# A graph attention network on one core: pauses ahead of every fifth gather, the carries moved by 32x32 transposes, merged loads, and the spread from two digits

## The chip, the cores and the metric

The kernel runs on one NeuronCore of a Trainium2 chip. The metric is the device time of one execution in microseconds, the median of the runs. The engines are PE (TensorE, with its weight loads shown as PEld), DVE (VectorE), ACT (ScalarE), POOL (GpSimd) and SP (SyncE, which only issues DMAs here).

## The reference

6250 nodes with 128 features and 206250 edges, sorted by destination (100000 edges both ways and a loop at each node). Three graph attention layers, then one layer of sums over edge attributes:

```python
xl = (x @ Wl + bl).reshape(n, heads, outc)
e_feat = leaky_relu(xl[src] + (x @ Wr + br).reshape(n, heads, outc)[dst], 0.2)
logits = einsum('ehc,hc->eh', e_feat, att)
m = segment_max(logits, dst);  a = exp(logits - m[dst])
out = segment_sum(xl[src] * a[:, :, None], dst) / segment_sum(a, dst)   # then bias, layer norm, relu
```

Two layers have four heads, the third one has one. The last part takes `segment_sum(edge_attr, col)` (96 wide), divides by the counts, joins it to the node's features, and applies two products with a batch norm between them. Both results are added to the input and normalized.

## The kernel before, in words

**Data.** The edges lie in 62 chunks of 3328, each of 26 tiles of 128 edges (`TILES`). An item is a chunk with a window of 128 destination nodes; a table made at the start (`item_tab`) lists them, 62 for each layer in this trace. Each layer has a node phase (it writes the tables `xl_tab` and `xr_tab` of 132 columns and the state) and an edge stage over the items. The stages lie at 132 to 2716, 2871 to 5359 and 5507 to 7998 us.

**An item.** GpSimd gathers 128 rows of `xl_tab` by source for each tile, 26 indirect DMAs (L633) of 66 KB each, into `xl_g`, which has two buffers. PE spreads the destinations of a tile over 128 partitions (L683: a row of `sel` picks tile t of `rel`, the destinations less the window's base, in bf16); ScalarE turns them into a one-hot tile `ST` (L879, L881) and, from the other side, `S` (L854, L857). PE multiplies `ST` by the window's `xr_w` (L694), VectorE adds the gathered rows (z, L1133), takes the relu times the attention vector (L1140), and sums per head (L1149, L1163): the logits.

**The maxima.** The logits are transposed (L701) so that each tile and head is one of 104 rows. Scans give the running maxima from both ends of a row (L1187, L1188). A segment can run through several tiles, so the last column of the upward and the first of the downward scan go through PE to one partition (L704, L705), two scans of 104 elements join them over the tiles (L1195, L1196) with penalties that ScalarE made from `tile_ends`, two sums give the carries (L1199, L1200), PE brings them back to 104 partitions (L708, L709), and VectorE copies them out of PSUM (L1206). They start the scans L1208 and L1210, whose result PE transposes (L712). Then come `shifted` (L1216), the exponential (L891), the messages (L1226) and their sums on PE (L727), and the merge into the state.

**Order.** Items are pipelined: a step of each engine opens one item (to its logits) and closes the one before it, and prepares the next. Groups of four tiles (`GROUPS`, seven of them, the last of two) interleave opening and closing: `runs` at group 0, `carries` and `maxima` at 1, `shift` at 2, `message` from 2 on (`SUMS_AT`). The order on each queue is written out by hand; semaphores join the queues.

**Waits of GpSimd.** The buffer of an item is free once the messages of the item two before it are made, group by group: GpSimd waits for `msg_done[g]` ahead of each group. Ahead of groups 1 to 6 it also pauses until all but the last gather of the group before have landed (`most_gathered`, L630). A small `sem_inc(spacer)` stands behind each wait.

**Loads.** SP loads for the item after the next (`load_item`, L515 to L530): three tables by partition (`idx`, `dst_e`, `dst_next`), the destinations by row four times (`dst_r`, one for each head), the ends of each tile, the window's node numbers, and `xr_w`.

Of the kernel before, what the change touches and what calls it, by code (L numbers as in the profile page):

```python
# [25 lines left out]
P = 128  # L26
# [21 lines left out]
NG = len(GROUPS)  # L48
SUMS_AT = {2: (0,), 3: (1, 2), 4: (3, 4), 5: (5, 6)}
EA_CUTS = (0, 4, 9, 16, TILES)  # L50
LH = TILES * HEADS

# [33 lines left out]
ITEM_DMAS = 5 + HEADS  # L86
# [3 lines left out]
def gnn_program(nc, x, src_t, dst_t, next_t, dst, edge_attr, node_id, Wl, bl, Wr, br, att, c, g, be,  # L90
                u, W1, b1, gamma, beta, W2, b2, out):
    ctx = ExitStack()
    with ctx:
# [16 lines left out]
        item_tab = scratch("item_tab", (MAX_ITEMS, 2), I32)  # L110

# [40 lines left out]
        idx = sb("idx", [P, 2, TILES], I32)  # L152
        dst_e = sb("dst_e", [P, 2, TILES], I32)
        dst_next = sb("dst_next", [P, 2, TILES], I32)
        dst_r = sb("dst_r", [LH, 2, P], I32)
        tile_ends = sb("tile_ends", [1, 2, TILES, 2], I32)
# [6 lines left out]
        rel = sb("rel", [TILES, 2, P], BF16)  # L163
        sel = sb("sel", [TILES, TILES, P], BF16)
        neg_p = sb("neg_p", [P, 1])
        distT = sb("distT", [P, 2, 4 * P])
# [7 lines left out]
        logit = sb("logit", [P, 2, LH])  # L174
        seg_last = sb("seg_last", [P, TILES])
        row_eq = sb("row_eq", [LH, P])
        row_pen = sb("row_pen", [LH, P + 1])
        tile_eq = sb("tile_eq", [1, TILES + 1])
        tile_one = sb("tile_one", [1, TILES])
        through = sb("through", [1, 2, TILES])  # L180
        through_pen = sb("through_pen", [1, 2, LH])
        enter_pen = sb("enter_pen", [1, 2, LH])
        run_up = sb("run_up", [LH, P])
        run_down = sb("run_down", [LH, P])
        open_max = sb("open_max", [1, 2, LH + 2])
        carry = sb("carry", [1, 2, LH])
        carry_col = sb("carry_col", [LH, 2])
        up = sb("up", [LH, P])
        seg_max = sb("seg_max", [LH, P])
# [56 lines left out]
        b_cut = s_flat[0:PARTS, F + 2 * b_all:F + 4 * b_all].bitcast(BF16)  # L246
        bn = sb("bn", [P, 8, 2])
# [5 lines left out]
        lt_ps = PS[0:LH, 4, 0:P]  # L253
        spread_ps = PS[:, 7, :]
        mb_ps = PS[:, 4, 128:128 + LH]
        open_ps = [PS[0:1, 4, 232 + d * LH:232 + (d + 1) * LH] for d in range(2)]
        carry_ps = PS[0:LH, 4, 440:442]
        agg_ps = PS[:, 5, 0:MSG]
        ea_ps = PS[:, 6, 0:D_EDGE]
        hT_ps = flat[:, 0:NROWS]  # L260
# [1166 lines left out]
```

## Time and profile before

| | us |
|---|---|
| median of 3 runs (lowest, highest) | 8285.53 (8282.69, 8302.3) |
| the profiled execution | 8275.22 |
| its span, first to last instruction | 8273.2 |
| PE busy | 5435.2 (66%) |
| POOL busy | 4817.3 (58%) |
| DVE busy | 4759.2 (58%) |
| ACT busy | 4443.8 (54%) |
| first gather | 131.9 |

Busy time is that of the instructions' records; waiting, register work and DMA issue are not counted. The gap behind a gather is therefore idle time, whatever it is for. A wait "<- remote" or "<- issue" is one whose release the records do not show; PE's own ends are modelled. A gather's record is the making of its descriptors on GpSimd, not the transfer. Matmuls of f32 data have two records each.

### The profile page before, as it was taken

To read this page: it belongs to the slowest core of one execution; us is meant where nothing else is said; L and a number is where in the kernel's file an instruction comes from. 1 tells how busy PE (TensorE), PEld (TensorE's weight loads), DVE (VectorE), ACT (ScalarE), POOL (GpSimd) and SP (SyncE) were. 2 spreads that over 40 slices of the span, in tenths; PEclk is the share of its full clock that TensorE was granted. 3 is DMA by queue.
4 is the path that set the end of the run, shared out by engine and by line. 5 is a ranking of instruction groups with operands and counts; after the bars stand their busy time and mean duration, and the time that the engine had idled before them with its cause. 6 is when DMAs were issued, how large, how long until landed. Compare 5 with 4: busy or idle time off the path is not lost.

```text
span 8273.2 us, 114570 instructions
## 1 busy us (share of the span) xinstructions
PE 5435.2 (66%) x30380; PEld 4591.5 (55%) x30380; DVE 4759.2 (58%) x13239; ACT 4443.8 (54%) x10857; POOL 4817.3 (58%) x4843
## 2 busy tenths in 40 slices
PE   5777777777777765666656665666566666566656
PEld 3666666666666455555555554535555555455544
DVE  3555565555565555656556655655556556565556
ACT  3555555555555454555555655545555556555546
POOL 2666666666666166666666666626666666666640
PEclk8777777777777666666666666656666666666666
DMA  4333333333332322222222222242222222222221
GB/s 115 86 84 84 85 85 84 78 90 77 84 92 76 89 53 53 53 52 51 53 53 53 54 53 52 49 88 53 52 54 54 53 54 53 53 50 53 53 49 47
DMA packets 469478, 538.50 MB, mean 65 GB/s; under 512 B 196815, under 2 KB 377749, under 8 KB 461495
## 3 DMA queue, kind: packets, MB, share of 16 engines
q0 software_dynamic: 154752, 327.15, 17.7%
q1 hardware_dynamic: 314679, 210.82, 9.7%
q8 instruction: 18, 0.29, 0.0%
q14 instruction: 29, 0.24, 0.0%
HBM read 485.07 MB, written 52.43 MB: 65 GB/s over the span
## 4 chain that ended last, share of the span: by engine, by line
another core or an unknown queue 20%; POOL 18%; issue 18%; DVE 15%; PE 14%; ACT 9%; DMA 5%; DVEq 0%; POOLq 0%; ACTq 0%; SPq 0%
POOL xl_g L633 18%; DMA xl_g<-xl_tab,idx 4%; PE PS L694 3%; PE PS L727 3%; ACT dist L854 3%; DVE z L1133 3%; DVE am L1140 2%; PE PS L666 2%; DVE msg L1226 2%; ACT distT L879 2%; PE PS L720 2%; DVE relu_logit L1149 1%; PE PS L683 1%; DVE relu_logit L1152 1%
## 5 line engine op out<-in xcount | busy, mean ns | idle before, releaser
L633 POOL DMA_INDIRECT xl_g<-xl_tab,idx x4836 | 4816.5, 996 | 3179.9 <-issue 2328.3
L727 PE MATMUL PS<-msg,S 128*128 128x137 f32 x9672 | 1699.2, 338 | 895.9 <-DVE msg L1226 588.1
L879 ACT ACTIVATE distT<-PS,neg_p 128x512 f32<-128x512 f32 x1302 | 847.1, 651 | 2521.4 <-remote 1821.0
L727 PEld LDWEIGHTS PS<-msg,S 128*128 128x128 f32 x9672 | 1530.5, 236 | 1022.8 <-issue 943.8
L694 PE MATMUL PS<-xr_w,ST 128*128 128x132 f32 x9672 | 2032.1, 373 | 86.0 <-DVE z L1133 44.4
L1133 DVE TENSOR_TENSOR z<-PS,xl_g 128x528 f32<-128x528 f32 x1302 | 863.6, 663 | 1977.4 <-remote 1251.5
L694 PEld LDWEIGHTS PS<-xr_w,ST 128*128 128x128 f32 x9672 | 1820.8, 275 | 153.6 <-issue 128.6
L854 ACT ACTIVATE dist<-node_row,neg_dst 128x128 f32<-128x128 f32 x4836 | 1534.5, 386 | 0.0
L683 PE MATMUL PS<-rel,sel 26*128 26x128 bf16 x4836 | 640.9, 267 | 1058.2 <-ACT distT L879 593.9
L683 PEld LDWEIGHTS PS<-rel,sel 26*128 26x128 bf16 x4836 | 348.5, 111 | 1348.4 <-ACT distT L879 675.5
L1140 DVE SCALAR_TENSOR_TENSOR am<-z,att_relu 128x512 f32<-128x512 f32 x1302 | 852.6, 655 | 6.5
L881 ACT ACTIVATE ST<-distT 128x512 f32<-128x512 f32 x1302 | 780.4, 599 | 41.6
L857 ACT ACTIVATE S<-dist 128x512 f32<-128x512 f32 x1302 | 780.4, 599 | 41.2
L1226 DVE TENSOR_TENSOR msg<-xl_g,msg 128x512 f32<-128x512 f32 x1302 | 791.2, 642 | 0.6 <-ACT msg L891 0.6
L1149 DVE TENSOR_REDUCE relu_logit<-am 128x16 f32<-128x512 f32 x868 | 554.1, 638 | 17.1
L720 PE MATMUL PS<-ea,S 128*128 128x96 f32 x3224 | 551.6, 336 | 5.6 <-issue 5.2
L720 PEld LDWEIGHTS PS<-ea,S 128*128 128x128 f32 x3224 | 512.3, 246 | 31.8 <-issue 24.1
L708 PE MATMUL PS<-ones,carry 1*104 1x1 f32 x372 | 88.0, 303 | 530.4 <-DVE carry L1200 294.2
L891 ACT ACTIVATE msg<-shifted 128x104 f32<-128x104 f32 x186 | 56.6, 304 | 622.0 <-DVE shifted L1216 361.7
L708 PEld LDWEIGHTS PS<-ones,carry 1*104 1x104 f32 x372 | 72.8, 250 | 570.4 <-DVE carry L1200 319.5
L1195 DVE TENSOR_TENSOR_SCAN open_max<-through_pen,PS 1x104 f32<-1x104 f32 x186 | 66.5, 357 | 493.7 <-remote 445.0
L1152 DVE TENSOR_REDUCE relu_logit<-am 128x4 f32<-128x512 f32 x434 | 276.9, 638 | 8.5
(198 smaller groups left out, 4005.1 us busy)
## 6 DMA issues: line engine op xcount, KB each, us to landing
xl_g<-xl_tab,idx POOLq DMA_INDIRECT x4836
ea<-edge_attr SPq DMA_DIRECT2D x62, 1248.0 KB
xr_w<-xr_tab SPq DMA_DIRECT2D x186, 66.0 KB
dst_r<-dst SPq DMA_DIRECT2D x744, 13.0 KB
node_row<-node_id SPq DMA_DIRECT2D x186, 64.0 KB
xl_tab<-xl_g SPq DMA_DIRECT2D x30, 330.0 KB, 3.7
xr_tab<-xl_g SPq DMA_DIRECT2D x30, 330.0 KB, 5.0
st_old<-state SPq DMA_DIRECT2D x124, 68.0 KB
```

The lines of the kernel that those rows point to most:

```text
L633: pool.indirect_dma_start(xl_g[:, q, t, :], None, xl_tab[:, :], bass.IndirectOffsetOnAxis(idx[:, q, t:t + 1], 0))\
L683: last = pe.matmul(spread_ps[:, n * P:(n + 1) * P], sel[:, t, :], rel[:, q, :], start=True, stop=True)
L694: last = pe.matmul(zp[(q + g) % 2][:, n, :], ST[:, t, :], xr_w[:, q, :], start=True, stop=True)
L720: pe.matmul(ea_ps, S[:, q, t, :], ea[:, q, t, :], start=t == 0, stop=t == TILES - 1)
L727: last = pe.matmul(agg_ps, S[:, q, t, :], msg[:, t, :], start=t == 0, stop=t == TILES - 1)
L854: last = act.activation(dist[:, (q + g) % 2, m, :], node_row[:, q, :], ACT.Abs, bias=neg_dst[:, q, t:t + 1])
L857: act.activation(S[:, q, GROUPS[g][0]:GROUPS[g][0] + n, :], dist[:, (q + g) % 2, 0:n, :], ACT.Relu, bias=1.0, scale=-1.0)\
L879: act.activation(distT[:, (q + g) % 2, 0:n], spread_ps[:, 0:n], ACT.Abs, bias=neg_p[:, 0:1]).then_inc(spread_read, 1)
L881: act.activation(ST[:, GROUPS[g][0]:GROUPS[g][-1] + 1, :].rearrange("p t n -> p (t n)"), distT[:, (q + g) % 2, 0:n], ACT.Relu, bias=1.0, s ...
L1133: dve.tensor_tensor(out=z[:, (q + g) % 2, 0:n, :], in0=zp[(q + g) % 2][:, 0:n, :], in1=xl_g[:, q, a:a + n, :], op=ALU.add).then_inc(z_done ...
L1140: dve.scalar_tensor_tensor(am[:, (q + g) % 2, 0:n, :], z[:, (q + g) % 2, 0:n, 0:F], 0.0, att_relu[:, stage, :].unsqueeze(1).to_broadcast([ ...
L1226: dve.tensor_tensor(out=msg[:, a:a + n, 0:F].rearrange("p t (h f) -> p t h f", h=HEADS), in0=xl_g[:, q, a:a + n, 0:F].rearrange("p t (h f) ...
```

## The change

It does six things together.

1. GpSimd waits for landed gathers ahead of tiles 5, 10, 15, 20 and 25 (`PACE = 5`) and not ahead of tiles 4, 8, ..., 24. The gathers are counted in ten sets (`SETS`) cut at both the pauses and the groups; each pause waits for the sets that end before the gather still in flight. The waits for messages stay ahead of tiles 0, 4, ..., 24. `dynamic_dma_scratch_size` is set to 8192 where the default was 16384.
2. The logits have 128 rows instead of 104 (32 for each head, the last six zero). The carries go by VectorE's 32x32 transposes: two of [128, 32] bring the ends to where each head's 26 tiles lie along a row, the scans and sums run over 26 elements on all partitions, and one of [128, 64] takes the carries back. PE's four products and the copy out of PSUM are gone.
3. The flags of tile ends come from `dst_r` by a copy and one transpose; `tile_ends` is gone.
4. The spread is one product for a group, of weights 128 and 1 (`digit_w`, 2x128) by two bf16 digits of the destinations (2x512). The digits are made for all edges at the start and stored in `digit_tab`; `sel` and `rel` are gone, and the window's base moves into the bias of L879 (`neg_node`).
5. The loads of an item are `edges` (three tables in one), `dst_r` (one table of 128 rows), `digits`, `node_row` and `xr_w`.
6. ScalarE makes the penalties in four activations, not five.

```diff
+PACE = 5
+PAUSES = range(PACE, TILES, PACE)
+STEPS = sorted({PACE * b - 1 for b in range(1, len(PAUSES) + 1)} | {g[-1] + 1 for g in GROUPS})
+SETS = [range(a, b) for a, b in zip([0] + STEPS[:-1], STEPS)]
+SET_OF = [m for m, tiles in enumerate(SETS) for t in tiles]
+PAUSE_FOR = {t: [m for m, tiles in enumerate(SETS) if max(t - PACE - 1, 0) <= tiles[-1] < t - 1] for t in PAUSES}
-                        for g, tiles in enumerate(GROUPS):
-                            pool.wait_ge(msg_done[g], pairs * (2 * stage) + 2 * i + (q + 1))
-                            pool.sem_inc(spacer, 1)
-                            if g:
-                                pool.wait_ge(most_gathered[g - 1], (pairs * (2 * stage) + 2 * i + (q + 1)) * (16 * (len(GROUPS[g - 1]) - 1)))
+                        v = pairs * (2 * stage) + 2 * i + (q + 1)
+                        for t in range(TILES):
+                            for m in PAUSE_FOR.get(t, ()):
+                                pool.wait_ge(gathered[m], v * (16 * len(SETS[m])))
                                 pool.sem_inc(spacer, 1)
-                            for t in tiles:
-                                pool.indirect_dma_start(xl_g[:, q, t, :], None, xl_tab[:, :],
-                                                        bass.IndirectOffsetOnAxis(idx[:, q, t:t + 1], 0))\
-                                    .then_inc(gathered[q][g] if g == NG - 1 or t == tiles[-1] else most_gathered[g], 16)
+                            if t % 4 == 0:
+                                pool.wait_ge(msg_done[t // 4], v)
+                                pool.sem_inc(spacer, 1)
+                            pool.indirect_dma_start(xl_g[:, q, t, :], None, xl_tab[:, :],
+                                                    bass.IndirectOffsetOnAxis(idx[:, q, t:t + 1], 0))\
+                                .then_inc(last_gathered[q] if SET_OF[t] == len(SETS) - 1 else gathered[SET_OF[t]], 16)
...
-                        for n, t in enumerate(GROUPS[g]):
-                            last = pe.matmul(spread_ps[:, n * P:(n + 1) * P], sel[:, t, :], rel[:, q, :], start=True, stop=True)
-                        last.then_inc(spread, 1)
+                        a, n = GROUPS[g][0] * P, len(GROUPS[g]) * P
+                        pe.matmul(spread_ps[:, 0:n], digit_w[:, :], digits[:, q, a:a + n], start=True, stop=True).then_inc(spread, 1)
...
+            dve.wait_ge(dst_in, 16)
+            dve.tensor_scalar(all_digit, all_dst, DIGIT.bit_length() - 1, None, ALU.arith_shift_right).then_inc(digits_made, 1)
+            dve.tensor_scalar(all_dst, all_dst, DIGIT - 1, None, ALU.bitwise_and).then_inc(digits_made, 1)
+            dve.wait_ge(digits_made, 2)
+            dve.tensor_copy(all_digits[0], all_digit).then_inc(digits_made, 1)
+            dve.tensor_copy(all_digits[1], all_dst).then_inc(digits_made, 1)
...
-                    first, last = tile_ends[:, q, :, 0], tile_ends[:, q, :, 1]
+                    dve.tensor_copy(ends[:, :, :], dst_r[:, q, 0:P:P - 1].unsqueeze(2).to_broadcast([P, 2, SQ])).then_inc(flag_done[2], 1)
+                    dve.wait_ge(flag_done[2], v * 3 - 2)
+                    dve.transpose(ends_T[:, :, :].rearrange("p a t -> p (a t)"), ends[:, :, :].rearrange("p a t -> p (a t)")).then_inc(flag_done[2], 1)
...
+                    dve.wait_ge(runs_done, v)
+                    dve.transpose(run_T[:, 0, :], run_up[:, P - SQ:P])
+                    dve.transpose(run_T[:, 1, :], run_down[:, 0:SQ]).then_inc(open_done, 1)
                     dve.wait_ge(open_done, v)
-                    dve.tensor_tensor_scan(open_max[:, 0, 1:LH + 1], through_pen[:, 0, :], open_ps[0], -BIG, ALU.add, ALU.max)
+                    dve.tensor_tensor_scan(open_max[:, 0, 1:TILES + 1], through_pen[:, 0, :], run_T[:, 0, 0:TILES], -BIG, ALU.add, ALU.max)
...
+                    dve.wait_ge(carry_done, v)
+                    dve.transpose(carry_T[:, :, :].rearrange("p a t -> p (a t)"), carry[:, :, :].rearrange("p a t -> p (a t)")).then_inc(carryT_done, 1)
...
-                    dve.tensor_copy(carry_col[:, :], carry_ps).then_inc(carrycol_done, 1)
...
-    nc = bacc.Bacc("TRN2", target_bir_lowering=False, num_devices=1)
+    nc = bacc.Bacc("TRN2", target_bir_lowering=False, num_devices=1, dynamic_dma_scratch_size=8192)
```

## Rows read from the trace of the kernel before

**Rows 1.** the cores: span and mean granted TensorE clock
```profile
core 0: 8273.2 us, clock 0.696
```

**Rows 2.** by stretch: PE, PEld, DVE, ACT, POOL busy, granted clock, DMA share, GB/s
```profile
132.00:2716.00 2584.00, 1908.96 (x11753) 1698.22 (x11754) 1457.05 (x4148) 1362.35 (x3325) 1602.16 (x1612) 0.76 0.32 84
2871.00:5359.00 2488.00, 1541.83 (x8606) 1315.33 (x8606) 1454.48 (x4044) 1404.28 (x3375) 1609.05 (x1612) 0.67 0.24 53
```

**Rows 3.** GpSimd's group of gathers: count, busy us, mean ns, idle and what ended it
```profile
L633 POOL DMA_INDIRECT xl_g<-xl_tab,idx x4836 | 4816.5, 996 | 3179.9 <-issue 2328.3 <-DMA xl_g<-xl_tab,idx 686.4 <-DVE msg L1226 165.2
```

**Rows 4.** GpSimd's waits (us, times, longest): first stage, second stage, whole run
```profile
POOL xl_g L633 <- DMA xl_g<-xl_tab,idx: 349.2, 202, 5.8
...
POOL xl_g L633 <- DMA xl_g<-xl_tab,idx: 176.7, 147, 2.8
...
POOL xl_g L633 <- DVE msg L1226: 165.2, 36, 15.9
```

**Rows 5.** timeline of GpSimd: start, us, instruction, idle before
```profile
4058.26 0.94 POOL L633 DMA_INDIRECT xl_g<-xl_tab,idx  x1 [0.30 <-issue]
4060.44 0.95 POOL L633 DMA_INDIRECT xl_g<-xl_tab,idx  x1 [1.23 <-DMA xl_g<-xl_tab,idx]
4062.52 0.95 POOL L633 DMA_INDIRECT xl_g<-xl_tab,idx  x1 [1.13 <-issue]
```

**Rows 6.** the chain of work in order of time, around one item's end
```profile
4079.23 0.02 POOLq L631
4079.25 0.76 issue
...
4080.74 0.02 POOLq L628
...
4082.75 0.02 POOLq L628
...
4083.01 1.01 POOL xl_g L633
```

**Rows 7.** groups by line and shape: VectorE around the carries, and its longest
```profile
L1133 DVE TENSOR_TENSOR z<-PS,xl_g 128x528 f32<-128x528 f32 x1116 | 783.8, 702 | 1811.6 <-remote 1108.2 <-DMA xl_g<-xl_tab,idx 409.9 <-PE PS L694 224.7
...
L1195 DVE TENSOR_TENSOR_SCAN open_max<-through_pen,PS 1x104 f32<-1x104 f32 x186 | 66.5, 357 | 493.7 <-remote 445.0 <-PE PS L705 26.3 <-issue 22.3
...
L1123 DVE TENSOR_SCALAR neg_dst<-dst_e 128x26 f32<-128x26 int32 x186 | 33.0, 177 | 0.0
...
L1206 DVE COPY carry_col<-PS 104x2 f32<-104x2 f32 x186 | 28.8, 155 | 120.4 <-remote 101.0 <-PE PS L709 13.4 <-issue 6.0
...
L1140 DVE SCALAR_TENSOR_TENSOR am<-z,att_relu 128x512 f32<-128x512 f32 x1302 | 852.6, 655 | 6.5
...
L1226 DVE TENSOR_TENSOR msg<-xl_g,msg 128x512 f32<-128x512 f32 x1302 | 791.2, 642 | 0.6 <-ACT msg L891 0.6
```

**Rows 8.** timeline of PE and VectorE, from the product to the scan
```profile
4024.22 0.55 PE L705 MATMUL PS<-ident,run_down 104*1 104x104 f32 x2
...
4033.66 0.36 DVE L1195 TENSOR_TENSOR_SCAN open_max<-through_pen,PS 1x104 f32<-1x104 f32 x1 [7.75 <-remote]
```

**Rows 9.** windows on GpSimd: gathers (x) between unplanned gaps of 1.13 us
```profile
3959.34:4062.52 103.18, 63.54 (x67) 0.68 0.23 52
4062.52:4160.02 97.50, 63.98 (x64) 0.68 0.25 54
4160.02:4259.23 99.21, 66.27 (x66) 0.72 0.24 52
```

**Rows 10.** timeline of VectorE and GpSimd, a message beside a gather
```profile
4073.62 1.28 DVE L1226 TENSOR_TENSOR msg<-xl_g,msg 128x512 f32<-128x512 f32 x2
...
4073.83 1.29 POOL L633 DMA_INDIRECT xl_g<-xl_tab,idx  x1 [1.38 <-DMA xl_g<-xl_tab,idx]
```

**Rows 11.** the copy at the start, and a store (KB, us to landing)
```profile
L1033 DVE CAST sel<-ident 26x3328 bf16<-26x3328 f32 x1 | 1.9, 1880 | 0.0
...
xr_tab<-xl_g SPq DMA_DIRECT2D x30, 330.0 KB, 5.0
```

More of the change, by code:

```diff
@@ L51 @@
 LH = TILES * HEADS
+SQ = 32
+LP = SQ * HEADS
 NB = 5
@@ L173, in gnn_program @@
         relu_logit = sb("relu_logit", [P, LH])
-        logit = sb("logit", [P, 2, LH])
+        logit = sb("logit", [P, 2, LP])
         seg_last = sb("seg_last", [P, TILES])
[L176 to L189, printed above, removed]
+        row_eq = sb("row_eq", [LP, P])
+        row_pen = sb("row_pen", [LP, P + 1])
+        ends = sb("ends", [P, 2, SQ])
+        ends_T = sb("ends_T", [P, 2, SQ])
+        tile_eq = sb("tile_eq", [P, TILES + 1])
+        tile_one = sb("tile_one", [P, TILES])
+        through = sb("through", [P, 2, TILES])
+        through_pen = sb("through_pen", [P, 2, TILES])
+        enter_pen = sb("enter_pen", [P, 2, TILES])
+        run_up = sb("run_up", [LP, P])
+        run_down = sb("run_down", [LP, P])
+        run_T = sb("run_T", [P, 2, SQ])
+        open_max = sb("open_max", [P, 2, TILES + 2])
+        carry = sb("carry", [P, 2, SQ])
+        carry_T = sb("carry_T", [P, 2, SQ])
+        up = sb("up", [LP, P])
+        seg_max = sb("seg_max", [LP, P])
         shifted = sb("shifted", [P, LH])
@@ L283, in gnn_program @@
         state_stored = sem("state_stored")
-        most_gathered = sems("most_gathered", NG - 1)
-        gathered = [sems(f"gathered{q}_", NG) for q in range(2)]
+        gathered = sems("gathered", len(SETS) - 1)
+        last_gathered = sems("last_gathered", 2)
         spacer = sem("spacer")
@@ L469, in _ @@
             sp.wait_ge(table_in, 16)
+            sp.wait_ge(digits_made, 4)
+            for w in range(2):
+                sp.dma_start(digit_tab[w].rearrange("c (h e) -> (c h) e", h=2), all_digits[w]).then_inc(digits_out, 16)
+            sp.wait_ge(digits_out, 32)
             pairs = sp.value_load(pairs_i[0:1, 1:2], min_val=MIN_PAIRS, max_val=MAX_PAIRS)
@@ L743, in pe_step @@
                                 spread_group(opens, g + 2)
-                        if closes and g == 0:
-                            close("open")
-                        if closes and g == 1:
-                            close("carry")
                         if closes and g == 2:
```

114 lines of the change are left out of this document (56 added, 58 removed).

## The prediction

> **What bounds the kernel now.** I read the clock and span first [rows 1], then busy time by stage [rows 2]. No engine is full: in the first edge stage PE is busy for 74% of the stretch, GpSimd for 62%. Busy time hides the bound here, because GpSimd's own gaps are part of its work. The group of gathers shows it [rows 3]: 4836 gathers of 0.996 us and 3179.9 us of idle time, of which only 165.2 us ended on VectorE's messages. So the third view is what GpSimd waits for [rows 4], and the fourth their order in time [rows 5, 6]. A gather follows the one before it after 0.30 us. At a pause (it waits until all but the last of the group's gathers have landed) the gap is about 1.13, at 4060.44 it is 1.23 us: 0.35 to 0.45 us until the wait has passed, then 0.76 us from there to the next gather. The reader is to see that a gather is 1.25 us of GpSimd whatever the data, that 26 of them and 6 pauses are 26 x 0.996 + 20 x 0.30 + 6 x 1.16 = 38.9 us, and that a stage of 2488 us is 62 such items of 40.1 us. GpSimd's issue is the bound. Other engines matter where they keep it waiting: 36 times, 4.6 us each, 15.9 us at most, nearly always ahead of an item's first gather [rows 4].
>
> **Pauses, six to five in an item.** Before, GpSimd waits ahead of tiles 4, 8, ..., 24; after, ahead of 5, 10, 15, 20, 25. Each still leaves one gather in flight, so each costs what it costs now. In stage 0, 202 gaps ended on a landing and lasted 349.2 / 202 = 1.73 us; the other 170 of its 62 x 6 pauses took 1.13 us; the mean is 1.46, so one pause less saves 1.16 us an item, 72 us in the stage. In stage 1, 147 gaps took 176.7 / 147 = 1.20 us and 225 took 1.13: 1.16, less 0.30 is 0.86 us, and 107 us for the 124 items of two such stages. Together **-179 us**; the low end is 186 x 0.83 = -154 (every pause at its shortest, 1.13 less 0.30). The message waits stay ahead of tiles 0, 4, ..., 24, and now mostly stand between two gathers with no pause beside them. Such a wait costs nothing if it has passed: at 4080.74 and 4082.75 two of them run beside the gathers of 4080.01 and 4081.26, and the next gather starts at 4083.01, 0.30 us behind the last one's end [rows 6]. That VectorE waits for two sets of gathers in three groups is a 0.05 us step beside idle time of its own (44% of stage 0, [rows 2]), so nothing; if that cover were gone it would be 0.15 us an item.
>
> **The carries.** Before, VectorE's two scans over the open runs wait for a PE product, the carries go back through PE, and a copy brings them out of PSUM. VectorE sat idle 493.7 us ahead of the scan at L1195, 2.65 us an item, and 120.4 us ahead of the copy at L1206, 0.65 us [rows 7]; in the item of [rows 8] the product's record ends at 4024.77 and the scan starts at 4033.66. After, VectorE transposes the ends itself: three transposes and 26-element scans and sums in place of 104-element ones. I price a transpose as the 128x26 operation at L1123, 0.18 us; three of these, two scans and two sums of about 0.2 are some 1.3 us against five operations of 0.16 to 0.36 us now, so VectorE's own work is unchanged and 3.3 us of waiting goes. The spread loses 19 of its 26 matmuls an item and PE's four carry products go; PE's results come late in such stretches (the 8.9 us above), so I add 1 us for the shorter queue, an estimate. GpSimd comes 0.96 us earlier. The first message is then 3.3 + 1 - 0.96 = 3.4 us earlier against the gather that waits for it. With 36 waits spread evenly from 0 to 9.2 us (mean 4.6), a share (1 - 3.4 / 9.2)^2 = 0.40 stays, so of the 154 us that they cost over a plain gap 0.6 goes: **-95 us**. Ends: -154 (all goes), and +35 (nothing goes and each wait grows by the 0.96 us that GpSimd is early). What is late next is GpSimd's own issue.
>
> **The smaller descriptor area.** The area for gather descriptors is set to 8192 bytes a partition, half of the default. The trace has gaps of 1.13 us behind a gather that is followed by no pause, as at 4062.52 [rows 5], and they come back every 64 to 67 gathers [rows 9]: 65 on average, of which the rows are three of the four that follow 3959.34. That does not fit the loop (52 gathers) but would fit an area that fills. 4836 / 65 is 74 of them. If half the area fills twice as often, 75 more come, of which a fifth fall on a pause and are hidden: 75 x 0.8 x 0.83 = **+49 us**. No row shows that the area is the cause; the ends are 0 and 75 x 0.83 = +62. I take the price, since the period has no other match.
>
> **The shared port.** Gathers of 0.95 us stretch where VectorE multiplies the messages, both inputs in SBUF: 1.29 us at 4073.83 beside L1226 [rows 10]. Over the run the stretch is 4816.5 - 4836 x 0.95 = 222 us, beside 791.2 + 852.6 us of the two such groups L1226 and L1140 [rows 3, 7], 0.14 for each us. The change adds some 0.9 us an item of SBUF-to-SBUF work (three transposes, the copy of the ends, two scans that read PSUM before): 186 x 0.9 x 0.14 = **+23 us**, ends 0 and +60 (the 0.34 us by which that gather grew are 0.36 us for each us of it, for all of the 167 us added). The Trainium skill, GPSIMD Engine Reference, section "Key points", says that GpSimd shares its SBUF interfaces with VectorE and contends with instructions in a 2-port mode or with two SBUF inputs. The trace agrees for two inputs (1.29 against 0.95 us); by the rule the transposes and copies might be free or dear according to their mode, which no row here shows, and the sum would lie between 0 and the +60 above. It speaks against this change.
>
> **Start and loads.** The load of all destinations, four VectorE operations over 1664 columns and two stores stand ahead of the first round. VectorE drops the 1.88 us copy of 3328 columns at L1033 [rows 11], about half of what it gains at the same rate (4 x 0.94 = 3.8), and waits for weights anyway. SP waits for stores of 413 KB, priced as the 330 KB store of 5.0 us [rows 11]: **+5 us**, ends 0 and +10. The item's loads fall from ten DMAs to five. They are issued an item ahead, so 40 us of gathers hide them before and after, nothing is gained; without that cover the 2 to 3 us that SP saves would count. ScalarE drops one of five small activations off the path.
>
> **Sum.** 8275.2 us (the profiled execution; span 8273.2 and 2.0 around it) - 179 - 95 + 49 + 23 + 5 = 8078. The median of the runs is 10.3 us above the profiled one: 8088, so I predict **8090 us**, 2.4% faster. With each doubtful term halfway to its ends, one or two at a time, this case covers 8030 to 8150.
>
> **Rivals.** *All waits go* (0.20): messages are never late, the area costs nothing, the port little: 8275 - 179 - 154 + 5 + 10 = 7957, up to 8030. For it: the carries' round trip is most of what delays them. Against: the longest wait is 15.9 us, more than any part removed. *Only the pause* (0.18): PE's lateness is not cured by removing round trips, because the lateness sits in the products that remain; the waits stay or grow: 8275 - 179 + 35 + 49 + 23 + 5 + 10 = 8218, from 8150. For it: z at L1133 also waits for PE after its record ends, and it stays (1108.2 us, [rows 7]). *Slower* (0.07): a message wait apart from a pause drains GpSimd's queue and costs the 0.76 us restart too. Tiles 4, 8, 12, 16 and 24 then add five gaps: 186 x 5 x 0.83 = +772, 8088 + 772 = 8860 us. It decides as soon as more than about 1.3 of these five restart in an item (the 195 us gained over 186 x 0.83). Against it: [rows 6], where two such waits pass under a gather; it is kept because no row shows three gathers, a wait and a pause in this order. *The gain is eaten* (0.05): port and area at their dear ends and waits that grow: 8275 - 154 + 35 + 62 + 60 + 10 + 10 = 8298, or within 0.3% of it. PE falling to its lower clock with less work (0.67 of full speed already in stage 1, [rows 2]) would act through late messages, so it is part of the second rival.
>
> **Numbers.** The forecast has 0.50. The range 7960 to 8200 holds it, nearly all of the first rival's and two thirds of the second's time, and leaves out about 0.2. A measurement of this kernel can tell 0.3% (25 us) from no change. Faster 0.88, same 0.05, slower 0.07.
>
> **What would show it.** Five gaps over 1 us in an item's gathers, ahead of the second gather of every fifth; items of stage 1 near 39.0 us; 0.30 us behind message waits; fewer than 25 waits on VectorE's message and under 80 us in them; the unplanned gaps every 32 or so gathers; gathers of 1.00 us on average; first gather 5 us later. It would go wrong if gaps stand at tiles 4, 8, 12 as well, if the message waits do not fall, or if the mean gather grows past 1.02 us.

## The result, and the profile of the changed kernel

| | before | after |
|---|---|---|
| median of 4 runs each, us | 8293.92 (8282.69 to 8314.43) | 8778.46 (8747.18 to 8810.17) |
| ratio, 95% interval | | 1.058 (1.054 to 1.062) |
| profiled span, us; granted clock | [rows 1] | 8745.1; 0.679 |

The change made the kernel 5.8% slower, where 2.4% faster was forecast; 8778 us lies far outside the range. I read the changed kernel in the order in which I read the one before. Its span and clock, against [rows 1]:

```profile
core 0: 8745.1 us, clock 0.679
```

Busy time by stretch (the two stretches of [rows 2] at their new places; PE, PEld, DVE, ACT, POOL, granted clock, DMA share, GB/s):

```profile
144.00:2862.00 2718.00, 1803.60 (x9991) 1556.46 (x9992) 1457.18 (x4366) 1319.16 (x3240) 1578.20 (x1612) 0.73 0.30 80
3029.00:5680.00 2651.00, 1482.44 (x6859) 1196.06 (x6859) 1447.25 (x4246) 1354.45 (x3267) 1582.97 (x1612) 0.65 0.22 50
```

Every engine has less to do or as much, and both stages are longer, by 134 and 163 us. So nothing became busier; something waits more. GpSimd's group, against [rows 3], and its waits over the whole run (us, times, longest), against [rows 4]:

```profile
L652 POOL DMA_INDIRECT xl_g<-xl_tab,edges x4836 | 4739.6, 980 | 3736.8 <-issue 2258.3 <-DVE msg L1250 979.9 <-DMA xl_g<-xl_tab,edges 495.9
...
POOL xl_g L652 <- DVE msg L1250: 979.9, 131, 18.3
```

The waits on VectorE's message went from 165.2 us in 36 to 979.9 in 131. The pauses are as the change says. The timeline of GpSimd shows them five gathers apart, each 1.1 to 1.2 us:

```profile
4068.57 0.94 POOL L652 DMA_INDIRECT xl_g<-xl_tab,edges  x1 [1.18 <-DMA xl_g<-xl_tab,edges]
4069.82 0.94 POOL L652 DMA_INDIRECT xl_g<-xl_tab,edges  x1 [0.30 <-issue]
...
4073.57 0.95 POOL L652 DMA_INDIRECT xl_g<-xl_tab,edges  x1 [0.30 <-issue]
4075.73 0.94 POOL L652 DMA_INDIRECT xl_g<-xl_tab,edges  x1 [1.21 <-issue]
```

In the kernel before they are four apart:

```profile
4004.02 0.94 POOL L633 DMA_INDIRECT xl_g<-xl_tab,idx  x1 [1.11 <-DMA xl_g<-xl_tab,idx]
...
4009.87 0.95 POOL L633 DMA_INDIRECT xl_g<-xl_tab,idx  x1 [1.08 <-DMA xl_g<-xl_tab,idx]
```

The message waits inside an item now mostly stand between two gathers that are 0.30 us apart (18 longer gaps away from the pauses, in 186 items), so the rival *Slower* with its five restarts an item did not happen. Summed over the gathers' starts and ends, the idle time inside the items fell by 230 us (2535 to 2305), the gathers themselves by 77 (4816.5 to 4739.6), and the idle time ahead of an item's first gather grew by 776 (514 to 1290). That one sum is the loss. (It has the turns between stages in it.) Who makes the first message late shows in VectorE's groups, by line and shape:

```profile
L1151 DVE TENSOR_TENSOR z<-PS,xl_g 128x528 f32<-128x528 f32 x1116 | 784.6, 703 | 2568.9 <-remote 2197.3 <-PE PS L712 186.4 <-DMA xl_g<-xl_tab,edges 97.8
...
L1219 DVE TENSOR_TENSOR_SCAN open_max<-through_pen,run_T 128x26 f32<-128x26 f32 x186 | 39.6, 213 | 6.3
```

The scan of the carries waits for nothing any more (493.7 us in [rows 7], 6.3 now). But z, the operation that takes PE's products out of PSUM, waits 2197.3 us for something called remote; for z at L1133 that was 1108.2 in [rows 7]. The timeline shows what it is:

```profile
4028.23 0.60 PE L702 MATMUL PS<-digits,digit_w 2*128 2x512 bf16 x1 [2.48 <-issue]
4028.89 2.13 PE L712 MATMUL PS<-xr_w,ST 128*128 128x132 f32 x8
...
4031.06 0.95 POOL L652 DMA_INDIRECT xl_g<-xl_tab,edges  x1 [1.15 <-issue]
...
4032.82 0.69 ACT L884 ACTIVATE distT<-PS,neg_node 128x512 f32<-128x512 f32 x1 [2.16 <-remote]
4032.85 0.71 DVE L1151 TENSOR_TENSOR z<-PS,xl_g 128x528 f32<-128x528 f32 x1 [3.23 <-remote]
```

PE's spread ends at 4028.83 and its eight products at 4031.02; ScalarE, which waits for the first, and VectorE, which waits for the second, both go on at 4032.8, 4.0 and 1.8 us later (ScalarE had been idle for the last 2.16 us of this), within 0.03 us of each other, and behind a pause of GpSimd. PE's results, or word of them, come late, and here two of them at once. It is the lateness of [rows 8] (8.9 us), which I had called PE's own. The chain of waits gives it a name of its own; by engine, of the changed kernel:

```profile
another core or an unknown queue 34%; DVE 20%; PE 16%; ACT 16%; issue 11%; POOL 1%; DMA 1%; DVEq 1%; SPq 0%; ACTq 0%; POOLq 0%
```

The program runs on one core, so no other core can release anything. The same line of the kernel before, which was there to be read before I predicted:

```profile
another core or an unknown queue 20%; POOL 18%; issue 18%; DVE 15%; PE 14%; ACT 9%; DMA 5%; DVEq 0%; POOLq 0%; ACTq 0%; SPq 0%
```

The word remote proves nothing by itself: it only says that no record names what released the instruction. That the results are late shows in the starts of what waits for them. Where ScalarE's distT had waited for more than 1 us, it started 2.5 us behind the end of the last product of the spread at the median in the kernel before, and 3.2 us in the changed one.

### The profile page after: what moved, and what is told of

The parts are those of the page before. It is cut to its first block, busy times and chain, and to the rows that moved or that the text cites. A ratio compares the mean times of both kernels' runs of the same rounds, so it can differ in the third digit from the quotient of the medians.

```text
span 8745.1 us, 105988 instructions
## 1 busy us (share of the span) xinstructions
PE 5223.6 (60%) x25358; PEld 4225.2 (48%) x25358; DVE 4790.9 (55%) x13989; ACT 4347.3 (50%) x10671; POOL 4740.5 (54%) x4843
## 3 DMA queue, kind: packets, MB, share of 16 engines
q0 software_dynamic: 154752, 327.15, 16.7%
## 4 chain that ended last, share of the span: by engine, by line
another core or an unknown queue 34%; DVE 20%; PE 16%; ACT 16%; issue 11%; POOL 1%; DMA 1%; DVEq 1%; SPq 0%; ACTq 0%; POOLq 0%
ACT dist L861 6%; PE PS L738 4%; ACT distT L884 4%; PE PS L712 4%; DVE z L1151 3%; DVE am L1158 3%; DVE msg L1250 3%; PE PS L731 3%; ACT ST L886 2%; PE PS L685 2%; DVE relu_logit L1167 2%; PE PS L702 2%; ACT S L864 1%; DVE relu_logit L1170 1%
## 5 line engine op out<-in xcount | busy, mean ns | idle before, releaser
L652 POOL DMA_INDIRECT xl_g<-xl_tab,edges x4836 | 4739.6, 980 | 3736.8 <-issue 2258.3
L884 ACT ACTIVATE distT<-PS,neg_node 128x512 f32<-128x512 f32 x1302 | 846.1, 650 | 3339.8 <-remote 2533.0
L738 PE MATMUL PS<-msg,S 128*128 128x137 f32 x9672 | 1733.6, 342 | 1121.1 <-DVE msg L1250 647.2
L738 PEld LDWEIGHTS PS<-msg,S 128*128 128x128 f32 x9672 | 1562.8, 240 | 1293.3 <-issue 1187.2
L702 PE MATMUL PS<-digits,digit_w 2*128 2x512 bf16 x1302 | 641.4, 493 | 1960.8 <-ACT distT L884 1110.4
L702 PEld LDWEIGHTS PS<-digits,digit_w 2*128 2x128 bf16 x1302 | 124.1, 95 | 2280.3 <-ACT distT L884 1250.7
L731 PEld LDWEIGHTS PS<-ea,S 128*128 128x128 f32 x3224 | 545.7, 261 | 41.7 <-issue 41.7
L1167 DVE TENSOR_REDUCE relu_logit<-am 128x16 f32<-128x512 f32 x868 | 556.5, 641 | 17.1
L1259 DVE TENSOR_SCALAR some<-PS 128x1 f32<-128x1 f32 x186 | 29.4, 158 | 461.3 <-remote 404.1
L1181 DVE TENSOR_TENSOR logit<-relu_logit,z 128x16 f32<-128x16 f32 x1302 | 228.8, 176 | 0.1
L685 PE MATMUL PS<-w_lr,n_hT 128*128 128x264 f32 x300 | 173.4, 678 | 0.0
```

The lines of the kernel that those rows point to most:

```text
L652: pool.indirect_dma_start(xl_g[:, q, t, :], None, xl_tab[:, :], bass.IndirectOffsetOnAxis(idx[:, q, t:t + 1], 0))\
L702: pe.matmul(spread_ps[:, 0:n], digit_w[:, :], digits[:, q, a:a + n], start=True, stop=True).then_inc(spread, 1)
L731: pe.matmul(ea_ps, S[:, q, t, :], ea[:, q, t, :], start=t == 0, stop=t == TILES - 1)
L738: last = pe.matmul(agg_ps, S[:, q, t, :], msg[:, t, :], start=t == 0, stop=t == TILES - 1)
L884: act.activation(distT[:, (q + g) % 2, 0:n], spread_ps[:, 0:n], ACT.Abs, bias=neg_node[:, q:q + 1]).then_inc(spread_read, 1)
```

## The experiments

The kernels of the experiments ran in five sessions, each on one chip, one kernel after the other. (The expectations call a session a call.) Ratios are to the kernel before, timed in the same session.

| session | kernel | median, us | ratio (95%) | waits on messages, us, times | PE's results |
|---|---|---|---|---|---|
| 1, before 8220 | b_area8192 | 8163 | 0.994 (0.992 to 0.996) | 0 | late |
| | b_pace5 | 8696 | 1.060 (1.056 to 1.065) | 805.9, 156 | late |
| | a_pace4 | 8354 | 1.018 (1.014 to 1.021) | 0 | late |
| | a_area16128 | 8517 | 1.036 (1.033 to 1.040) | 749.8, 98 | late |
| 2, before 8063 | b_nopause | 9794 | 1.214 (1.208 to 1.220) | 2804.0, 209 | late |
| | b_memset4 | 8625 | 1.068 (1.064 to 1.072) | 859.1, 115 | late |
| | b_pace3 | 8435 | 1.045 (1.040 to 1.050) | 0 | late |
| | b_pace5_half | 8668 | 1.074 (1.069 to 1.080) | 923.5, 157 | late |
| 3, before 8099 | b_pace5_area8192 | 7897 | 0.975 (0.973 to 0.977) | 0 | prompt |
| | b_skip4_area8192 | 8024 | 0.992 (0.990 to 0.993) | 0 | prompt |
| | b_memset4x2 | 8230 | 1.017 (1.015 to 1.018) | 0 | prompt |
| | a_pace4_spread | 8170 | 1.009 (1.008 to 1.011) | 0 | prompt |
| 4, before 8095 | r_after | 7735 | 0.956 (0.954 to 0.957) | 0 | prompt |
| | r_b_pace5 | 7905 | 0.977 (0.975 to 0.978) | 0 | prompt |
| | r_b_pace5_area8192 | 7904 | 0.976 (0.975 to 0.978) | 0 | prompt |
| | r_before (one run) | 8109 | | 0 | prompt |
| 5, before 8225 | a_pace6 | 9059 | 1.102 (1.095 to 1.110) | 1425.0, 176 | late |
| | a_pace8 | 9401 | 1.142 (1.135 to 1.149) | 1952.4, 194 | late |

The last column is explained under session 4. "b_" are made from the kernel before, "a_" from the changed one, "r_" are the same kernels once more.

### Session 1: which part of the change

**b_area8192**: the kernel before, with

```diff
-    nc = bacc.Bacc("TRN2", target_bir_lowering=False, num_devices=1)
+    nc = bacc.Bacc("TRN2", target_bir_lowering=False, num_devices=1, dynamic_dma_scratch_size=8192)
```

> The kernel before with the descriptor area set to 8192 and nothing else changed. Three theories stand. A, pacing: TensorE's results come late only while GpSimd makes gathers, the pauses let it catch up, and fewer pauses make it later; the area does nothing here: 8294 us, within 0.3%. B, area: the smaller area is what slows TensorE's results and SyncE's issue: near 8750 us, with over 100 waits of GpSimd on VectorE's message, and stage 1's blocks of 20 matmul passes at 8 us in place of 5. C, the rest of the change (spread, carries, loads): 8294 us. The term of the prediction (unplanned gaps twice as often) is a fourth reading: 8343 us, with gaps of 1.13 us every 32 gathers. I expect A or C, so no change.

0.994. Neither 8750 nor the 8343 of my own term: the unplanned gaps of [rows 9] are gone altogether, and instead the pauses ahead of tiles 4 to 20 last 1.28 to 1.84 us on average. No message is waited for: an item's first gather starts 16.7 us behind the end of the message at the median, 8.0 us in the first trace of the kernel before.

**b_pace5**: the kernel before, with the changed kernel's pauses, sets and waits, and nothing else of it.

```diff
+PACE = 5
-                            if g:
-                                pool.wait_ge(most_gathered[g - 1], ...)
+                            for m in PAUSE_FOR.get(t, ()):
+                                pool.wait_ge(gathered[m], v * (16 * len(SETS[m])))
```

> The kernel before with only the pauses moved: GpSimd waits ahead of tiles 5, 10, 15, 20, 25 in place of 4, 8, ..., 24, with the new sets of semaphores; carries, spread, loads and area as before. Theory A (pacing): one pause less makes TensorE's results later by more than it saves GpSimd: slower, 8500 to 8750 us, with 90 or more waits on VectorE's message. Theory B (area) and C (the rest): the pause saves its 179 us and little is given back: 8110 to 8180 us.

1.060: the whole loss, from the pauses alone. This is the experiment that decides what in the change is slow. Its waits on messages:

```profile
POOL xl_g L640 <- DVE msg L1235: 805.9, 156, 16.7
```

**a_pace4**: the changed kernel, with

```diff
-PACE = 5
+PACE = 4
```

> The changed kernel with PACE 4: pauses ahead of tiles 4, 8, ..., 24 as before, all else as changed. Theory A (pacing): TensorE catches up again, the message waits fall to 36 or fewer, and the time is 8294 less the gain of the carries: 8180 to 8300 us. Theory B (area) and C (the rest): one more pause on top of what was lost: 8780 plus up to 180, so 8800 to 8950 us.

1.018. The message waits vanish, as pacing has it, and 4% come back. It stays 2.3% above b_area8192, which has the same six pauses and the same area, so with six pauses the rest of the change costs time in session 1. The largest piece of it is the pause ahead of tile 4, 1.99 us on average against 1.33; no trace shows why.

**a_area16128**: the changed kernel with `dynamic_dma_scratch_size=16128`.

> The changed kernel with a descriptor area of 16128 bytes a partition, near the default of 16384 (80 bytes too many to fit beside the new buffers). Theory A (pacing) and C (the rest): 8780 us, within 0.5%. Theory B (area): back to what was forecast, 8050 to 8200 us, with fewer than 36 waits on VectorE's message.

1.036: slow like b_pace5, with 98 message waits. Against b_pace5 of the same session it is 2.1% faster (8517 to 8696), so with five pauses the carries, spread and loads do gain something in session 1. Against the first result (1.058) the large area looks 2% better, but the changed kernel itself was not in session 1.

### Session 2: what in a pause does it

**b_nopause**: each group's gathers count on one semaphore of their own, and GpSimd waits for no landing.

```diff
-                            if g:
-                                pool.wait_ge(most_gathered[g - 1], ...)
-                    dve.wait_ge(gathered[q][g], use * (16 if g < NG - 1 else 16 * n))
+                    dve.wait_ge(gathered[q][g], use * (16 * n))
```

> The kernel before with no pause at all: GpSimd waits for messages and never for landings (each group's gathers have a semaphore of their own in either half of the pair, which VectorE waits for). Its own work falls to 26 x 0.996 + 25 x 0.30 = 33.4 us an item, 6.3 us less than now. If the pauses are what lets TensorE's results through, these come later still than with five pauses: over 150 waits on VectorE's message, and 9000 us or more. If the run length between pauses has nothing to do with it and five pauses were a bad place for another reason, the gain of the shorter items shows: 8000 us or less.

1.214, with 2804 us of message waits: each item is 5.4 us shorter by itself and waits about 15 us for its message.

**b_memset4**: as b_nopause, and ahead of tiles 4, 8, ..., 24

```diff
+                                pool.memset(pause[:, :], 0.0).then_inc(paused, 1)
+                                pool.wait_ge(paused, ...)
```

> The kernel before, where ahead of tiles 4, 8, ..., 24 GpSimd waits for no landing; it writes one column of its own (a memset of 128 x 1) in that place and waits for that. So GpSimd stops making descriptors for about as long, but whatever has landed doesn't matter. If a stop of GpSimd is enough: within 1% of the kernel before, 8220 to 8300 us. If the gathers must have landed (their transfers are what holds TensorE's results off): as slow as with five pauses or slower, 8700 us or more.

1.068. But the stops lasted 0.93 us and not 1.13, so the run doesn't tell a short stop from a missing landing.

**b_pace3**: b_pace5 with `PACE = 3`.

> The kernel before with a pause ahead of every third gather (eight in an item), in the form of the changed kernel. GpSimd's own item grows to 26 x 0.995 + 17 x 0.30 + 8 x 1.2 = 40.6 us. If shorter runs of gathers let TensorE's results through, no wait on VectorE's message is left, TensorE's updates come 1 us or less late on average in stage 1 (2.35 now, 2.83 with five pauses), and the time is 186 x 40.9 + 660 = 8270 us, within 1%. If run length isn't what matters, the message waits stay near 36 (165 us) and it is 8400 us.

No message is waited for, as expected, but 8435 us is dearer than the 8270 expected: the eight pauses make an item 40.2 to 40.3 us in the last two stages and 43.4 in the first.

**b_pace5_half**: b_pace5 with 66 columns in each gather in place of 132. The table is taken as one of twice as many half rows and the indices stay, so the kernel sums other data; it serves for its time alone.

```diff
-  pool.indirect_dma_start(xl_g[:, q, t, :], None, xl_tab[:, :],
+  pool.indirect_dma_start(xl_g[:, q, t, 0:XW // 2], None, xl_tab.rearrange("n (w f) -> (n w) f", w=2),
```

> The kernel before with five pauses, each gather fetching 66 of the 132 columns (half of the bytes, as many descriptors; the other half of the rows isn't fetched, so the sums are of other data). If the bytes of the gathers hold TensorE's results off: near the kernel before, 8300 us or less, with under 40 waits on messages. If it is that GpSimd makes descriptors, or how many there are: within 1% of the kernel with five pauses, 8650 to 8750 us.

1.074, 8668 us. The gathers' queue moved 163.73 MB in place of 327.15, and nothing got faster: halving the bytes doesn't let PE's results through.

The ratios of session 2 may be too high as a price of the late condition. The kernel before took 8063 us here, which is what it takes where PE's results are prompt (8099 and 8095 us in sessions 3 and 4; 8220 to 8294 in the sessions with late ones), and it has no trace there.

### Sessions 3 and 4: the same kernels the other way round

**b_pace5_area8192**: b_pace5 with the area of b_area8192. **b_skip4_area8192**: b_area8192 without the pause ahead of tile 4.

```diff
-                            if g:
-                                pool.wait_ge(most_gathered[g - 1], ...)
+                            for m in ((), (), (0, 1))[g] if g < 3 else (g - 1,):
+                                pool.wait_ge(most_gathered[m], ...)
```

**b_memset4x2**: b_memset4 with two waited memsets in each place. **a_pace4_spread**: a_pace4 with the 26 spread matmuls of the kernel before.

> The kernel before with both the five pauses and the area of 8192, carries, spread and loads as before. The two alone gave 1.060 and 0.994 of the kernel before. If they only add up: 1.054. If the small area costs what it cost in the changed kernel (1.058 against 1.036 with the large one): 1.08. If the small area heals here too, as it did with six pauses (no message wait left), 1.00 to 1.03.

> The kernel before with the area of 8192, without the pause ahead of tile 4: five pauses in an item, as in the changed kernel, but ahead of 8, 12, 16, 20 and 24, so that ten gathers follow one another across the start of an item and four elsewhere. If the number of pauses decides: as slow as the other kernel with five pauses and this area. If the slack left with six pauses and this area (GpSimd ready 16 us behind the message at the median) is what counts, and any placing will do: no message waits, and an item 0.8 to 1.0 us shorter than with six, 0.975 of the kernel before.

> As the kernel with one waited memset in place of each landing wait (stops of 0.93 us, 115 waits on messages, 1.068), but with two of them, so that each stop lasts 1.2 to 1.5 us, longer than the 1.13 of a pause on landings. If the length of the stop is what lets TensorE's results through: near the kernel before or better, 0.99 to 1.01, message waits under 100 us. If landings are what counts: still 1.05 or more, with message waits over 500 us.

> The changed kernel with PACE 4 and the old spread (26 matmuls an item from the selection rows, the digits not loaded per item; their tables are still made at the start). With the digits it was 1.0175 of the kernel before, while the kernel before with this area alone is 0.994, and neither waits for messages. If the digits' spread or its load is what makes the items longer (39.95 us against 39.28): 0.995 to 1.00. If it is the carries or the merged loads: 1.015 to 1.02, and the pause ahead of tile 4 still takes 1.99 us.

0.975, 0.992, 1.017 and 1.009. None of my readings had 0.975 for the first. In all four "another core or an unknown queue" is gone from the chain, and so are the message waits, so the session told nothing on placing, stops or spread as I had meant it: what these were to cure was not there. Two things can be read all the same. The pause of 1.96 us ahead of tile 4 is there in a_pace4_spread, so it comes of neither the digits nor the lateness. And five pauses are not the same wherever they stand: b_skip4_area8192 takes 127 us more than b_pace5_area8192, and 111 us of it are longer gaps between gathers inside the items. Chip, session and area were confounded, so the next session ran known kernels side by side.

> The changed kernel once more, beside the three that follow. In the traces so far TensorE's semaphore updates come 0.9 to 3.1 us late on average in ten kernels and 0.03 to 0.05 us late in four, and the four shared one chip. If the lateness is the chip's and not the kernel's, all traces of this call show it or none does. With it: 1.05 to 1.06 of the kernel before. Without it nothing delays the messages, no wait on a message is left, and the shorter items show: 186 x 38.1 + 700 = 7800 us, 0.96 to 0.98.

> The kernel before with only the five pauses, once more (1.060 on a chip where TensorE's updates come late). With late updates in this call: 1.05 to 1.07. Without: 0.96 to 0.98, with no wait on a message.

> The kernel before with five pauses and the area of 8192, once more (0.975 on a chip where no update comes late). If the updates come late in this call and the area does no more than the 0.6% it did with six pauses: 1.05 to 1.06. If the area cures the lateness at five pauses: 1.00 or less. Without late updates in this call: 0.97 to 0.98 again.

> The kernel before itself, for its trace on this chip: whether its updates come late (2.35 us on average in the first trace) and how many waits on messages it has (36, 165 us in the first). With late updates: 8200 to 8300 us, 25 or more such waits. Without: no such wait, items of 39.2 to 39.6 us in the second and third edge stage, 8050 to 8110 us.

**r_after** is the changed kernel to the letter, and it is 4.4% faster than the kernel before: 0.956 (0.954 to 0.957). b_pace5, 1.060 in session 1, is 0.977 here, on the same chip as in session 1. The area makes no difference (0.977 and 0.976). So the sign of the result hangs on a condition that no line of the kernels sets and that was the same in all traces of a session. The same kernel before, in its two traces, shows it; r_before, the scan of the carries and z, against L1195 and L1133 of [rows 7] (493.7 us, 445.0 of it remote; 1108.2 remote):

```profile
L1133 DVE TENSOR_TENSOR z<-PS,xl_g 128x528 f32<-128x528 f32 x1116 | 787.0, 705 | 2624.1 <-DMA xl_g<-xl_tab,idx 2595.0 <-PE PS L694 27.9
...
L1195 DVE TENSOR_TENSOR_SCAN open_max<-through_pen,PS 1x104 f32<-1x104 f32 x186 | 65.9, 354 | 45.1 <-PE PS L705 44.0 <-issue 0.5
L1206 DVE COPY carry_col<-PS 104x2 f32<-104x2 f32 x186 | 28.1, 151 | 3.2 <-PE PS L709 3.2
```

and the product and its scan in the timeline, against the 8.9 us of [rows 8]:

```profile
4023.46 0.34 PE L705 MATMUL PS<-ident,run_down 104*1 104x104 f32 x2
...
4024.74 0.35 DVE L1195 TENSOR_TENSOR_SCAN open_max<-through_pen,PS 1x104 f32<-1x104 f32 x1
```

Same work, same place: the scan waited 2.65 us an item in the first trace, and 0.24 us here. Nothing is remote; z waits for the gathers, as it should in a kernel that GpSimd bounds. The chain of waits of the two kernels in session 4, by engine, r_before and then r_after:

```profile
DMA 35%; POOL 33%; issue 24%; PE 4%; DVE 2%; ACT 1%; POOLq 1%; SPq 0%; DVEq 0%; ACTq 0%
```

```profile
DMA 33%; issue 30%; POOL 29%; PE 4%; DVE 2%; ACT 1%; POOLq 1%; SPq 0%; DVEq 0%; ACTq 0%
```

And r_after's span, GpSimd's group, and its first two stages:

```profile
core 0: 7731.6 us, clock 0.737
...
L652 POOL DMA_INDIRECT xl_g<-xl_tab,edges x4836 | 4670.8, 966 | 2797.8 <-issue 1619.9 <-DMA xl_g<-xl_tab,edges 1177.9
...
140.00:2568.00 2428.00, 1710.41 (x10104) 1503.98 (x10105) 1480.82 (x4411) 1334.35 (x3283) 1569.81 (x1612) 0.81 0.33 90
2716.00:5019.00 2303.00, 1405.99 (x6940) 1155.83 (x6940) 1473.19 (x4291) 1373.74 (x3313) 1550.20 (x1612) 0.71 0.25 58
```

I call PE's results late or prompt by two marks that split the twenty traces without a case between. In the eight of sessions 3 and 4 no wait of any engine is put down to remote; in the other twelve there are waits of this kind in each, least in b_pace3, with 265.1 us of distT and 8.3 of z. And the trace of the kernel before holds 51,280 records of semaphore updates in the first result and 138,636 in session 4, the changed kernel's 46,481 and 125,083; over all, 45,000 to 78,000 stand against 125,000 and more. Where records are missing, the averages in my expectations (updates 0.9 to 3.1 us late) may have counted the wrong ones. The starts of the waiting instructions don't have that fault. Where distT had waited for more than 1 us, it starts this long behind the end of the last product of the spread, at the median: 0.04 us in r_before, r_b_pace5 and r_after; in late traces 0.14 us with eight pauses (b_pace3), 2.5 with six (the kernel before), 3.3 with five (b_pace5) and 5.4 with none (b_nopause).

What waits for VectorE is not late in either condition. In both traces of the kernel before, PE's sums of messages begin 0.15 us behind VectorE's multiplication at the median, and ScalarE's exponential 0.03 us behind VectorE's subtraction.

Such starts also crowd behind the stops of GpSimd. In b_pace5 distT began 519 times after more than 1 us of waiting, 373 times within 3.6 us of the start of a stop of GpSimd of 0.8 us or more. In r_b_pace5, the same kernel with prompt results, it was 103 of 339. That speaks for stops that let held results through; it doesn't prove it, since an item's work also has a fixed place against the pauses.

### Session 5: fewer pauses

**a_pace6** and **a_pace8**: the changed kernel with `PACE = 6` (four pauses) and `PACE = 8` (three).

> The changed kernel with PACE 6: four pauses in an item, ahead of tiles 6, 12, 18 and 24. Two theories. That updates come late is a condition that lasted over whole calls, not part of a kernel: where updates come at once, a pause is pure cost and each left out saves 0.85 us an item, so 7735 - 186 x 0.85 = 7575 us, 0.936 of the kernel before, with no wait on a message; where they come late, each pause left out costs more than it saves, 1.08 or more with over 130 such waits. The rival: five pauses are just enough for TensorE in either condition, and with four the messages come late even where updates are recorded at once: 0.97 or more.

> The changed kernel with PACE 8: three pauses, ahead of tiles 8, 16 and 24. Where updates come at once: 7735 - 186 x 1.7 = 7420 us, 0.917 of the kernel before; GpSimd is then ready 4 us earlier against the message than with five, out of the 15 us that were left, so still without a wait on a message. Where they come late: 1.12 or more, on the way to the 1.21 of the kernel with no pause. The rival (pauses are needed in either condition): 0.97 or more.

The session fell into the late condition (35% of either chain has an unknown releaser): 1.102 and 1.142, as the first theory has it for that case. What fewer pauses do with prompt results was not seen; that the rival is wrong there is not shown. With late results the message waits by the number of landing pauses in an item now make a row of their own, over several kernels, sessions and chips: 0 us with eight; 0, 0 and 165.2 with six; 749.8 to 979.9 with five; 1425.0 with four; 1952.4 with three; 2804.0 with none. The two zeros with six pauses are b_area8192 and a_pace4, both with the small area. b_memset4, with six shorter stops and no wait for landings, has 859.1.

## Why the prediction was wrong

**The step that failed** is the one under the carries: the first message comes 3.4 us earlier, so of the waits' 154 us 0.6 goes, -95, with +35 as the dear end. It measured +786 (979.9 - 131 x 0.30, less 165.2 - 36 x 0.30). The 3.3 us of waiting did go, and the price of a transpose was right (0.17 to 0.25 us, 0.18 said). What I left out is that PE's results, in the condition in which both kernels ran, hang on GpSimd's stops, so that the term before it, one pause fewer, also moves this one. b_pace5 shows the sign: alone it costs 6.0% in that condition, and a_pace4, the changed kernel with its sixth pause back, waits for no message. My second rival had put the lateness in the products that remain, which is where it sits, but priced it as the 0.96 us by which GpSimd is early, and so got 8218.

**The pauses**, -179: near, and partly by luck. Inside the items 230 us of idle time went in the first result; in session 4 the pauses alone took 186 us out of the items (2535 to 2348) and 190 us off the time (0.9765 of 8095). But 61 of these 186 us are the unplanned gaps, which I had in another term with the other sign. The gaps at the pauses themselves gave 126 us, less than the low end of 154: the one ahead of tile 10 lasts 1.79 us in r_b_pace5. (In the first result they gave 198.)

**The smaller area**, +49: wrong. In session 4 the two kernels with five pauses differ by 1 us. The unplanned gaps of [rows 9] don't come twice as often with half of the area. The kernel before has 71 of them, 61 us in r_before, and they are gone with the small area (b_area8192) as well as with five pauses and the default one (r_b_pace5). What they are stays open. In session 1 the small area went with 0.6% less time at six pauses, 57 us, about the size of these gaps; but the pauses were longer in that trace, so that this is the reason is not shown.

**The shared port**, +23: wrong in sign. The gathers' own time fell by 77 us in the first result and by 148 in session 4. What I took for a rate is at least in large part a matter of phase. In r_before two multiplications of messages often run back to back over the start of the gather of tile 23, and it takes 1.67 us in place of 0.94 (1.6 us or more in 122 of 186 items):

```profile
4010.62 1.27 DVE L1226 TENSOR_TENSOR msg<-xl_g,msg 128x512 f32<-128x512 f32 x2
4011.05 1.67 POOL L633 DMA_INDIRECT xl_g<-xl_tab,idx  x1 [0.30 <-issue]
```

On average over the 186 items the gather of tile 23 takes 1.46 us there, 1.66 with the pauses alone (r_b_pace5), and 0.95 in r_after, where the same multiplications fall elsewhere. That one gather is 0.7 us an item, 130 of the 134 us between r_b_pace5_area8192 and r_after (4805 to 4671). The trace agrees with the rule on two SBUF inputs (the Trainium skill, GPSIMD Engine Reference, "Key points"): this stretch stands beside such an operation. It doesn't say by how much a gather grows, and here that depends on where it starts.

**Start and loads**, +5: the first gather came 12 us later in the first result and 2 us later in session 4.

**The carries with prompt results**: there were no message waits to shorten (in r_before an item's first gather starts 17.1 us behind the message at the median), so their gain of -95 isn't there either. Yet r_after is 2.1% faster than the pauses and area alone: that is the 130 us of the one gather and 41 us of shorter gaps at the pauses, and the carries and the spread were priced for neither. In session 4 the sum is -226 (gaps in the items), -148 (gathers) and -1 (ahead of the first gather), -375 in all, 8106.6 to 7731.6. That is twice the forecast gain, in a condition that the forecast didn't know of, and it doesn't bear the forecast out. Of the signs that I had named, the five gaps an item, the 0.30 us behind message waits and the few message waits are met there; an item of the second stage takes 37.1 us where 39.0 was said.

**What stays open**: what the condition is. It came and went on one chip (late in session 1, prompt in 4, late in 5), all kernels traced in one session were in the same condition, and nothing in a kernel turned it on or off. That it holds for a session as a whole is not shown: the kernel before was fastest of all in session 2 (8063 us), where its companions had late results. The granted clock is lower in the late traces; whether that follows from the waiting or is part of the condition is not shown. The recording of the runs is a rival that no run leaves out: the late traces hold fewer records of landed transfers too (34,948 against 114,211 for the kernel before), and every timed run has such a recording, so no time stands without one. Nor is it shown by what path GpSimd's gathers hold PE's results off; halving the bytes doesn't help (b_pace5_half), and a stop without a landing wasn't told apart (b_memset4 and b_memset4x2 fell into different conditions).

## What to carry to other kernels

A stop of an engine that makes descriptors is not only that engine's own time: before you price it by its gap, look whether other engines are released behind it. When the chain of waits of a one-core program gives a fifth of its length to an unknown releaser, as here, the times may come from a condition that is another in the next session; run both kernels again then before believing a few per cent of either sign. A chain without this share is no proof of the other condition: b_area8192, a_pace4 and b_pace3 had none of it and were late. For a kernel that has to do well in both conditions, the kernel before with the small area is the safe one of those tried (0.994 with late results; with prompt ones it was not timed), the changed kernel the fast one (0.956) only where they are prompt.

## What the runs showed of the hardware that was not expected

- The same kernel, unchanged, on the same chip: 1.060 and 0.977 of its baseline in two sessions (b_pace5). The changed kernel: 1.058 and 0.956.
- In the late condition the waits behind PE grow as GpSimd stops less: distT starts 0.14 us behind the spread with eight stops an item and 5.4 with none (medians), and the message waits go from 0 to 2804 us. With prompt results no message is waited for with five stops or six (r_b_pace5, r_before); each of the five costs 0.85 to 1.49 us over a plain gap.
- In the same traces, what waits for VectorE is not late (0.15 and 0.03 us in both conditions).
- The granted clock is lower where there is more waiting: the changed kernel's mean is 0.679 of full speed in 8745 us and 0.737 in 7732, the kernel before's 0.696 and 0.727.
- One gather of 26, beside two back-to-back multiplications of VectorE with both inputs in SBUF, takes 1.67 us in place of 0.94.
